# Two heads side by side or one head by pairs of key chunks: the order of attention in an eight-core, three-stage layer

## The reference

```python
# dense attention: 16 heads of 64
dist = clip(|i - j|, 0, 16);  scores = (q . k) * rel_emb[dist]
attn = softmax(where(causal, -inf, scores) / 8)
x = layernorm(x + (attn @ v) @ Wo + bo)
# two layers
h = shift_token(x); q, k, v = split(h @ wqkv)
q, k = rotary_xpos(l2norm(q) * qs, l2norm(k) * ks)
x = x + local_attention(q, k, v, window=512) @ wo
x = x + (a * gelu(g)) @ w2 + b2      # a, g from layernorm(shift_token(x)) @ w1 + b1
# and a last layernorm with the residual
```

## Time and profile before

| what | value |
|---|---|
| time, median of 2 runs | 5863.23 us (5860.74 to 5865.73) |
| time of the profiled execution | 5898.29 us |
| its span on the slowest core (core 7) | 5895.9 us |
| spans of the 8 cores | 5817.5 to 5895.9 us |
| mean granted TensorE clock, cores 0 to 3 / 4 to 7 (medians) | 0.646 / 0.637 |
| busy: PE / DVE / ACT / POOL | 53% / 29% / 19% / 7% |

### The profile page before, as it was taken

One profiled execution on the slowest core, in us unless ns is written; L12 is line 12 of the kernel. 1 busy time (PEld: TensorE's weight loads), 2 busy tenths in 40 slices (PEclk: granted clock), 3 DMA queues, 4 the chain that ended last, 5 costly groups with the idle time before them and its releaser, 6 DMA issues.

```text
span 5895.9 us, 37474 instructions; the slowest of 8 cores (5817.5 to 5895.9 us)
## 1 busy us (share of the span) xinstructions
PE 3140.5 (53%) x10393; PEld 1096.7 (19%) x10393; DVE 1727.6 (29%) x2540; ACT 1148.0 (19%) x1917; POOL 385.9 (7%) x868
## 2 busy tenths in 40 slices
PE   4456556456546411453255099982453354179961
PEld 2111211211211100211111033430111111034420
DVE  2222221221221354223323611114223323711116
ACT  1233234224324200221121010101121122010100
POOL 0000000000000000110011000000010011000000
PEclk8655655565555555556655578996555655589985
DMA  2000000000000021001000033331001100033431
GB/s 73 8 1 8 8 1 1 15 1 1 8 1 1 0 79 35 1 1 43 15 1 8 4 53 59 65 68 35 6 1 28 30 1 8 0 53 68 70 89 64
DMA packets 44573, 148.27 MB, mean 25 GB/s; under 512 B 16802, under 2 KB 17222, under 8 KB 37714
## 3 DMA queue, kind: packets, MB, share of 16 engines
q0 software_dynamic: 22080, 86.10, 8.6%
q1 hardware_dynamic: 22290, 59.78, 3.1%
HBM read 205.89 MB, written 16.78 MB: 38 GB/s over the span
## 4 chain that ended last, share of the span: by engine, by line
PE 45%; DVE 21%; DMA 15%; ACT 8%; issue 7%; POOL 2%; DVEq 1%; ACTq 0%; SPq 0%; POOLq 0%
PE PS L141 45%; ACT POOL L165 5%; DVE RS L146 5%; DMA POOL<-SQT 4%; DMA RS<-RS 4%; DVE RS L174 4%; DMA POOL<-POOL 3%; POOL POOL L146 2%; ACT RS L165 2%; DVE POOL L146 2%; DVE XT L146 2%; DVE SQT L146 1%; DVE PS L146 1%; DVE SQT L174 1%; DVE RS L152 1%
## 5 line engine op out<-in xcount | busy, mean ns | idle before, releaser
L141 PE MATMUL PS<-POOL 128*65 128x512 bf16 (+7 forms) x2176 | 956.6, 492 | 511.8 <-POOL POOL L146 428.0
L141 PE MATMUL PS<-HF,WBQ 128*128 128x512 bf16 (+1 forms) x3840 | 979.1, 417 | 269.9 <-DVE RS L146 128.1
L165 ACT ACTIVATE POOL<-PS,SMALL 128x512 bf16<-128x512 f32 (+3 forms) x1088 | 683.8, 635 | 1176.2 <-PE PS L141 1117.4
L141 PE MATMUL PS<-POOL,SMB 2*64 2x512 bf16 (+1 forms) x192 | 113.9, 593 | 1355.3 <-DMA POOL<-SQT 745.5
L141 PEld LDWEIGHTS PS<-HF,WBQ 128*128 128x128 bf16 (+1 forms) x3840 | 391.9, 105 | 838.3 <-issue 542.7
L146 POOL TENSOR_TENSOR POOL<-POOL,SMB 128x128 bf16<-128x128 bf16 x704 | 298.8, 424 | 2960.0 <-ACT POOL L165 2959.5
L141 PEld LDWEIGHTS PS<-POOL 128*65 128x65 bf16 (+1 forms) x2176 | 245.7, 115 | 1237.8 <-issue 1228.3
L174 DVE COPY RS<-PS 1x512 f32<-1x512 f32 (+1 forms) x288 | 197.3, 685 | 928.4 <-PE PS L141 789.4
L141 PE MATMUL PS<-POOL,WB 64*128 64x512 bf16 x1024 | 432.4, 609 | 12.0 <-DVE POOL L146 12.0
L146 DVE TENSOR_TENSOR XT<-PS,XT 128x512 f32<-128x512 f32 (+1 forms) x288 | 216.3, 751 | 584.7 <-PE PS L141 584.7
L146 DVE TENSOR_TENSOR POOL<-PS,RS 64x512 bf16<-64x512 f32 (+1 forms) x216 | 195.1, 903 | 616.7 <-PE PS L141 409.7
(11 more groups left out here) (68 smaller groups left out, 1443.4 us busy)
## 6 DMA issues: line engine op xcount, KB each, us to landing
WBQ<-w1P POOLq DMA_DIRECT2D x88, 512.0 KB, 5.4
WBQ<-w2P POOLq DMA_DIRECT2D x32, 704.0 KB, 6.7
XT<-xT SPq DMA_DIRECT2D x1, 8192.0 KB
x1spill<-XT SPq DMA_DIRECT2D x8, 1024.0 KB
POOL<-POOL SPq DMA_DIRECT2D x64, 128.0 KB
RS<-x1spill SPq DMA_DIRECT2D x8, 1024.0 KB
outT<-XT SPq DMA_DIRECT2D x8, 1024.0 KB
WBQ<-wqkvP POOLq DMA_DIRECT2D x12, 512.0 KB, 5.2
```

What stands on the lines that cost most here:

```text
L141: return eng.matmul(out, lhsT, rhs, start=start, stop=stop)
L165: return eng.activation(out, in_, func, **kw)
```

## The change

- `attn_group` takes one head at a time. Its chunks go in pairs: the scores of two chunks fill both banks of one PSUM tensor, one exp covers both (up to 1024 columns, from the first chunk's first column), then the fixes of both chunks, then S of the next first chunk, the two AV matmuls, and S of the next second chunk. The probability tiles alternate by pair. Each of the four heads has a context bank of its own.
- The normalization runs once per query tile for four heads (rows of 4 x 512) instead of once per pair of heads.
- The triangle multiplies (`bU`, `tc`, `tw`) go from GpSimd to the vector engine.
- In the dense stage, q and k of every group are projected ahead of its attention, q and k matmuls alternating over c, with two PSUM banks each; the second q and k buffers, `drive` and the yields go. All four weight loads are issued at the head of the group.
- The score bound is computed after the v projection instead of in between; 4 squarings instead of 8, over four PSUM banks.
- `bo` is no longer added to `XT` at the start: it is staged as two bfloat16 rows and added by one more matmul per output block in the first dense group (32 in all).
- `local_bias` is emitted after the v projection instead of ahead of it.

```diff
-        for hp in range(0, nh, 2):
-            pair = [hp] if hp + 1 >= nh else [hp, hp + 1]
-            emit_S(pair[0], 0)
-            for ci in range(nch):
-                if len(pair) > 1:
-                    emit_S(pair[1], ci)
-                emit_rest(pair[0], ci)
-                if ci + 1 < nch:
-                    emit_S(pair[0], ci + 1)
-                if len(pair) > 1:
-                    emit_rest(pair[1], ci)
-                yield
...
+        for hh in range(nh):
...
+            npairs = nch // 2
+            for b in range(npairs):
+                c0, c1 = 2 * b, 2 * b + 1
+                if b == 0:
+                    emit_S(0)
+                emit_S(c1)
+                kcA, cminA, cmaxA, _, _ = chunks[c0]
+                atile = v.AT if (b % 2 == 0) else v.AT2
+                ares = "AT0" if (b % 2 == 0) else "AT1"
+                p.act(atile[:, cminA:1024], g.ps[0][:, cminA:1024], AF.Exp,
+                      bias=biasap, scale=lay["scale"](g),
+                      reads=[psr(0, 0), psr(0, 1), lay["bias_res"]] + lay["scale_res"],
+                      writes=[ares], tag=nm + "exp")
+                fixes(c0, atile[:, 0:512], ares)
+                fixes(c1, atile[:, 512:1024], ares)
+                if b + 1 < npairs:
+                    emit_S(2 * b + 2)
+                for ci in (c0, c1):
+                    kc, cmin, cmax, kind, tcol = chunks[ci]
+                    p.mm(ctx_ps[:, cmin:cmax], v.VB[:, kc, 65 * hh:65 * hh + 65],
+                         atile[:, 512 * (ci % 2) + cmin:512 * (ci % 2) + cmax],
+                         ci == 0, ci == nch - 1,
+                         reads=[ares, "VB"], writes=[psr(*ci_bank)], tag=nm + "AV")
...
     for grp in range(2):
         local_qk_prep(p, g, v, l, grp, "q")
         local_qk_prep(p, g, v, l, grp, "k")
-        local_bias(p, g, f"lb{l}{grp}")
...
     for d in range(8):
         p.copy(g.HF[:, d, 1:S + 1], g.XT[:, d, 1:S + 1], reads=[f"XT{d}"],
                writes=[f"HF{d}"], tag="hf0")
-        p.ts(g.XT[:, d, 1:S + 1], g.XT[:, d, 1:S + 1], g.SMALL[:, 10, d:d + 1],
-             ALU.add, reads=[f"XT{d}", "SMa10"], writes=[f"XT{d}"], tag="addbo")
+    vff = pool_ffn(g)
+    bo_bf = vff.ST[:, 0:1024]
+    bohl = stage_bias_hilo(p, g, g.boH, bo_bf, "MCst", 512, "bo")
```

More of the change, by code:

```diff
@@ L479, in stage_bias_hilo, with bias_bounds @@
     return dst_bf[0:2, 0:2 * nseg]
[L482 to L498, removed]
-            yield
+def bias_bounds(p, g, QB, KB, mode, tag):
+    for which, buf, res in (("q", QB, "QB"), ("k", KB, "KB")):
+        for m in range(2):
+            p.tt(g.SQT[:, :], buf[:, m, :], buf[:, m, :], ALU.mult,
+                 reads=[res], writes=["SQT"], tag=tag + "sq")
+            for t4 in range(4):
+                i, half = 2 + t4 // 2, t4 % 2
+                p.mm(g.bank(i, half)[0:4, :],
+                     g.SMB[:, 4, 0:8].rearrange("p (a b) -> p a b", a=2)[:, m, :],
+                     g.SQT[:, 512 * t4:512 * t4 + 512], m == 0, m == 1,
+                     reads=["SQT", "SMB4"], writes=[psr(i, half)], tag=tag + "n2")
+        for t4 in range(4):
+            i, half = 2 + t4 // 2, t4 % 2
+            col = t4 if which == "q" else 4 + t4
+            p.red(g.SMALL[0:4, 2, col:col + 1], g.bank(i, half)[0:4, :], ALU.max,
+                  reads=[psr(i, half)], writes=[f"n2m{col}"], tag=tag + "n2m")
     p.red(g.SMALL[0:4, 2, 8:9], g.SMALL[0:4, 2, 4:8], ALU.max,
@@ L614, in attn_group @@
             if g.cfg.get("skip_norm"):
+                p.copy(v.CTX[0:64, hh, :], ctx_ps[0:64, :], reads=[psr(*ci_bank)],
+                       writes=[f"CTXn{hh}"], tag=nm + "cp")
                 continue
[L616 to L622 removed]
@@ L649, in attn_group @@
-            yield
+            p.copy(g.RS[64:65, 1, 0:512], ctx_ps[64:65, :], reads=[psr(*ci_bank)],
+                   writes=["sumrow"], tag=nm + "sum")
+            p.dma("sync", g.RS[0:4, 2, 0:512][hh:hh + 1, :], g.RS[64:65, 1, 0:512],
+                  ["sumrow"], [f"sspr{hh}"], tag=nm + "spr")
+        if g.cfg.get("skip_norm"):
+            continue
+        p.ts(g.RS[0:4, 3, 0:512], g.RS[0:4, 2, 0:512], 1e-30, ALU.max,
+             reads=[f"sspr{h}" for h in range(nh)], writes=["RS3"], tag=nm + "smx")
@@ new lines, in attn_group @@
+        for hh in range(nh):
+            ci_bank = 1 + hh // 2, hh % 2
+            p.mm(g.bank(3, 1)[0:64, :], g.SMB[0:2, 0, 0:64], atv[0:2, hh, 0:512],
+                 True, True, reads=[v.RHL_res, "SMB0"], writes=[psr(3, 1)], tag=nm + "rm")
+            p.copy(g.RS[0:64, 3, 0:512], g.bank(3, 1)[0:64, :], reads=[psr(3, 1)],
+                   writes=["RS3"], tag=nm + "rme")
+            p.tt(v.CTX[0:64, hh, :], g.bank(*ci_bank)[0:64, :], g.RS[0:64, 3, 0:512],
+                 ALU.mult, reads=[psr(*ci_bank), "RS3"], writes=[f"CTXn{hh}"],
+                 tag=nm + "cn")
@@ L1088, in local_phase @@
                    bo=False)
-        for _ in attn_group(p, g, v, lay):
-            pass
+        attn_group(p, g, v, lay)
 def ffn_phase(p, g, l):
```

334 lines of the change are left out of this document (122 added, 212 removed).

## The result

| what | before | changed |
|---|---|---|
| median | 5855.77 us (10 runs, 5843.15 to 5968.4) | 5951.80 us (11 runs, 5943.44 to 6046.44) |
| ratio | | 1.0177, 95% interval 1.0135 to 1.022 |
| profiled execution | 5898.29 us | 5980.2 us |

What follows compares the result with a forecast made beforehand. Latency in the chunk and normalization loops was taken as the bound, with no engine full in attention. Dense +183 and local -6 gave +177 us: 5863 + 177 = 6040 us against the median, range 5950 to 6190.

Steps and rivals of the forecast that it cites:

- two loops: In attention before the change: the chunk loop, 1.10 us per chunk of one head, and normalization, 44.7 us per query tile.
- change of shape: On PE where S and AV matmuls alternate: a step taken as 0.55 us, against 0.43 between matmuls of one shape.
- diag pair: Dense chunk pair with serial fixes bG, bE and triangle: 5.42 us for a head's first, 5.52 for its second.
- plain pairs: Dense chunk pairs without fixes, all steps in series: 3.62 us each against 2.21 before.
- corner pairs: Dense chunk pairs, one per head from the second query tile on: 3.87 us each.
- local pairs: Chunk pairs in local attention, four per head after the first query tile: 3.29, 3.28, 3.29 and 3.08 us.
- the gap: Between the chunk loops of successive query tiles, normalization and output matmuls included: one of about 32 us per tile.
- Slower by over 2%: Outcome for the whole kernel: a time above 5980 us, given a chance of 0.78.
- pairs closer than 3.3 us: Sign in the profile after: the forecast is wrong if pairs of exps stand closer than 3.3 us.
- Weights loaded ahead: Rival, S/AV loop on PE: the new order hides weight loads, 83 us less, 5957 us; chance 0.13.
- Dearer chain: Rival, chunk loop: triangle multiply costs 0.31 us (+56) and AV after AV 0.55 (+65), 6161 us; chance 0.18.
- Upper clock: Rival, attention: TensorE is granted 2.4 GHz, 499 us saved, 5541 us; chance 0.05.

## Why the prediction came out as it did

**What bounds the kernel: right.** Latency in two loops, at a clock of 0.50, before and after. That PE's busy time in the fourth group stayed (212 us for 219) while the group grew by 14% bears it out.

**The chunk loop: mechanism right, waits too long.** Exp 1.22 (measured 1.21; 1.12 in local), AV after AV 0.43, change of shape 0.55 (0.53 and 0.57), triangle 0.23 (0.225) all held. Mis-sized were the waits between ACT and DVE:
- bE to triangle: 0.20 taken from POOL's and bG's, 0.10 measured; triangle to the next bG: +0.10 taken, -0.09 measured; exp to the first bG of a second diag pair: 0.24 taken, 0.17 measured in all 64. A diag pair was 0.38 or 0.47 too dear: 128 of them, 54 us. The bounds given to this term (-30) didn't reach it; the overlap of two operations on DVE was not thought of.
- plain pairs 0.06 (144, 9 us), corner pairs 3.66 for 3.87 (48, 10 us).
- local pairs 3.15, 3.17, 3.15, 2.95 for 3.29, 3.28, 3.29, 3.08. Timeline of the changed kernel, core 1: the exp ends at 2651.59, the triangles start 0.10 later, where 0.24 was taken, and the two take 0.56 together: they write one tile, and stand 0.10 apart instead of overlapping.

```profile
2650.47 1.12 ACT L165 ACTIVATE POOL<-PS,SMALL 128x1024 bf16<-128x1024 f32 x1 [2.04 <-PE PS L141]
2651.69 0.56 DVE L146 TENSOR_TENSOR POOL<-POOL,SMB 128x128 bf16<-128x128 bf16 x2 [2.60 <-ACT POOL L165]
2653.64 1.12 ACT L165 ACTIVATE POOL<-PS,SMALL 128x1024 bf16<-128x1024 f32 x1 [2.04 <-PE PS L141]
```

The 0.24 came from the earlier trace rows, where it is the wait of bG, a DVE operation that reads the scores in PSUM, and was carried over to one that reads SBUF. bG still shows it in the first diag pair of the changed kernel (exp's end at 1999.66, bG at 1999.90); the triangle does not. Whether PSUM is the reason wasn't tried: cG and the bG of second diag pairs, which read PSUM too, start 0.17 after their exp.

Of the 61 us too much in the dense part, diag, plain and corner pairs hold 73; the gap, 0.7 too cheap in 16 query tiles, takes 11 back, the start and `bo` 6. That leaves 5 unassigned. The local groups were forecast 6 us each too long, with four 24 us; and the local group taken as a pattern from before, 302.4, was the longest of four (mean 300.7), which gives 7 back: -22 instead of -6.

**Normalization once: right.** 37 us of gain in each of eight groups by the run that undoes it; its 29.7 us a tile was 30.4 (32.5 less the head transition of 2.13).

**Projections, v, bound, start: right to about 1 us.** The loads of weights were hidden, as the prediction had it. **bo:** 21.6 us for 17 (first against second group), 0.67 a matmul instead of 0.53, over the upper of its two bounds (0.43 and 0.60). **local_bias:** nothing, as predicted.

**Slower by over 2%: given too much.** The measured value is 1.8%, and 0.78 stood on the other side of it. The error of each wait was small, 0.1 to 0.2 us, but nearly all had one sign, since they came from one group of rows, and they stand in 352 pairs. Errors of one source don't average out: the diag and local pairs came out 54 and 24 us too dear, where the range of the waits was 30 us each way. And the sign "pairs closer than 3.3 us" can hold for dense pairs alone: local ones were forecast at 3.08 to 3.29 and stand at 2.95 to 3.17.

**The rivals.** *Weights loaded ahead* gave 5957 us, 5 from the measured time, and is wrong all the same: S to AV and AV to S still cost 0.53 and 0.57. The Trainium skill ("TensorE: Matmul & The Clock Gate", part 2, on LDWEIGHTS) has loads pulled ahead of matmuls in flight where the row groups don't conflict or the load goes to the background weight buffer; the traces here show it between equal shapes, where the second AV comes 0.43 after the first, and not between the two shapes. *Dearer chain:* no, AV after AV is 0.43 and the triangle 0.225. The form of 58 cycles and the columns over the factor in the Trainium skill ("VectorE: DVE Perf Modes", section on the TRN2 errata) gave an estimate of 0.13 us; the trace doesn't agree (0.225). It does agree with an estimate of 0.22 from the roughly 150 cycles of start that the same section reports. *Upper clock:* no, 0.50 in every attention window.

**What was not asked.** The prediction costed the new loop as given and got the groups to 2 to 4%. It did not ask how much of the 1.35 us that a plain pair loses against two heads in turn (2.21 before, 3.56 after) hung on one line. Its own terms had the answer: 0.55 + 0.43 + 0.55 + 0.71 stood between exp and exp only because the second score stood behind the AV.

## What to carry to other kernels

An exp over two banks waits for both scores (3.56 us a pair against 2.16 with two exps, in the same order of matmuls). Before two small operations are merged, see whether the last of their inputs stands, in the queue of the engine that makes it, behind something that waits for the operation ahead: here 0.24 us of saved exp time cost 1.4 us a pair. Emit what the next step needs ahead of what consumes this one. And a near-zero total may be two large opposite terms (-453 and +556 here): run the change without its suspected part before anything else.

## What was not expected of the hardware

- Two DVE operations that share no tensor, one behind the other, overlap: the second starts 0.09 us before the first ends (2000.82 + 0.23 against 2000.96). Two that write one tile, the triangles of a local pair, stand 0.10 apart.
- The wait from ACT to DVE is not one number: 0.24 us ahead of the bG of a first diag pair, 0.17 ahead of that of a second and of cG, 0.10 ahead of the triangle.
- A DMA's issue on POOL's queue behind compute can cost far more than the compute: with two loads behind four triangles of 0.42 us ACT stood idle for 14.80 us, and for 2.69 with the triangles elsewhere.
- Two exps of 512 columns back to back take 1.45 us, one of 1024 takes 1.21: a merge saves 0.24 us and no more.
